# Early blocks of a routed expert network on one NeuronCore: two buffers for gathered rows and y, a ScalarE share of the rounding of h, copies of x one by one, other split of the early one-hots

## The reference

```python
z = _L0_cond_ref(x, cond_1024, L0_cond_weight)
logits = jnp.einsum('bsd,de->bse', z, Wr) + br
route_w = jax.nn.softmax(logits, axis=-1)
_, topk_idx = jax.lax.top_k(route_w, 2)
mask = jax.nn.one_hot(topk_idx, 8).sum(-2)
routed = route_w * mask
routed = routed / routed.sum(axis=-1, keepdims=True)
h = jax.nn.relu(jnp.einsum('bsd,edh->ebsh', z, W1) + b1[:, None, None, :])
expert_out = jnp.einsum('ebsh,ehd->ebsd', h, W2) + b2[:, None, None, :]
return x + jnp.einsum('bse,ebsd->bsd', routed, expert_out)
```

## Time and profile before

| what | value |
|---|---|
| median of 3 runs | 955.36 us |
| the profiled execution, its own time | 954.25 us |
| its span, first to last instruction | 952.4 us |
| PE busy | 891.8 us (94%) |
| DVE busy | 760.1 us (80%) |
| ACT busy | 560.0 us (59%) |
| POOL busy | 550.3 us (58%) |
| mean granted TensorE clock | 0.973 |

### The profile page before, as it was taken

How to read it: one execution, slowest core, us unless ns; L and a number is a source line. 1 busy time by engine, 2 the same in 40 slices (tenths; PEclk the granted TensorE clock), 3 DMA queues, 4 the chain that set the end, 5 groups by cost and what they waited for, 6 DMA issues and landing times.

```text
span 952.4 us, 20965 instructions
## 1 busy us (share of the span) xinstructions
PE 891.8 (94%) x6510; PEld 881.9 (93%) x6510; DVE 760.1 (80%) x1476; ACT 560.0 (59%) x971; POOL 550.3 (58%) x469
## 2 busy tenths in 40 slices
PE   4982799999999999999999999999999999999993
PEld 4981799998999999999999999999999999999993
DVE  3776589898998787887887878878878878888783
ACT  5854455557875655655656556556556565565561
POOL 6877154444444545665765656656657656566572
PEclk9995799999999999999999999999999999999997
DMA  7894845853443454423433343344234334244231
GB/s 247 286 335 182 287 102 111 252 134 79 96 128 91 90 134 91 85 48 89 89 85 94 49 95 83 45 94 88 47 88 89 56 82 90 51 89 88 46 45 22
DMA packets 52071, 104.25 MB, mean 109 GB/s; under 512 B 7104, under 2 KB 34272, under 8 KB 51264
## 3 DMA queue, kind: packets, MB, share of 16 engines
q0 software_dynamic: 27360, 38.36, 23.9%
q1 hardware_dynamic: 20544, 61.09, 19.5%
q10 hardware_dynamic: 4128, 4.33, 1.4%
HBM read 75.78 MB, written 36.35 MB: 118 GB/s over the span
## 4 chain that ended last, share of the span: by engine, by line
PE 81%; DVE 6%; DMA 4%; issue 3%; POOL 3%; ACT 1%; ACTq 1%; SPq 0%; DVEq 0%; POOLq 0%
PE psum L1412 13%; PE psum L1427 13%; PE psum L1426 13%; PE psum L1425 13%; PE psum L1414 12%; PE psum L1413 12%; PE psum L1391 2%; DMA z_row<-z_rows,idx_early 2%; POOL row_hot L532 1%; DMA x_buf<-in_xT 1%; DVE w_lo L1204 1%; PE psum L1309 1%; PE psum L1311 1%; PE psum L1310 1%; DVE h_hi L1245 1%
## 5 line engine op out<-in xcount | busy, mean ns | idle before, releaser
L764 ACT ACTIVATE h<-psum,b_all 128x384 f32<-128x384 f32 x376 | 218.0, 580 | 313.3 <-PE psum L1414 245.1
L1425 PE MATMUL psum<-w_hi,h_hi 128*128 128x256 f32 x1128 | 316.8, 281 | 4.6 <-DVE h_lo L1247 4.6
L1427 PE MATMUL psum<-w_hi,h_lo 128*128 128x256 f32 x1128 | 318.6, 282 | 0.0
L1426 PE MATMUL psum<-w_lo,h_hi 128*128 128x256 f32 x1128 | 316.9, 281 | 0.0
L1412 PE MATMUL psum<-z_hi,w_hi 128*128 128x384 f32 x752 | 259.0, 344 | 2.5 <-DVE z_lo L1210 2.0
L575 POOL DMA_INDIRECT out<-y,idx_put x102 | 226.1, 2216 | 49.1 <-POOL idx_put L571 26.7
L1414 PE MATMUL psum<-z_hi,w_lo 128*128 128x384 f32 x752 | 253.5, 337 | 0.0
L1413 PE MATMUL psum<-z_lo,w_hi 128*128 128x384 f32 x752 | 253.2, 337 | 0.0
L1204 DVE TENSOR_TENSOR w_lo<-raw,w_hi 128x1024 fp32r<-128x1024 f32 x190 | 232.7, 1225 | 22.8 <-ACT w_hi L705 22.7
L1247 DVE TENSOR_TENSOR h_lo<-h,h_hi 128x384 fp32r<-128x384 f32 x376 | 210.2, 559 | 13.0
L1425 PEld LDWEIGHTS psum<-w_hi,h_hi 128*128 128x128 f32 x1128 | 213.3, 189 | 6.6 <-DVE h_lo L1247 6.6
(11 more groups left out here) (198 smaller groups left out, 744.2 us busy)
## 6 DMA issues: line engine op xcount, KB each, us to landing
raw<-in_experts SPq DMA_DIRECT2D x64, 512.0 KB, 4.3
x_buf<-in_xT SPq DMA_DIRECT2D x16, 512.0 KB, 7.2
d_rep<-d_rows SPq DMA_DIRECT2D x4, 1056.0 KB, 7.0
z_rows<-z_all ACTq DMA_DIRECT2D x2, 2112.0 KB, 11.8
z_rows<-z_all SPq DMA_DIRECT2D x1, 2112.0 KB, 12.2
z_rows<-z_once SPq DMA_DIRECT2D x1, 2112.0 KB, 10.1
out<-y,idx_put POOLq DMA_INDIRECT x102, 4.7
z_row<-z_rows,idx_get POOLq DMA_INDIRECT x99
```

The costliest lines, as they stand in the source:

```text
L764: act.activation(h[c % NHP][:], h_ps[c % HP][:, 0:TB], ACT.Relu, bias=b1_all[:, ds(e, 1), c]).then_inc(s_relu, 1)
L1425: pe.matmul(yp, hi, w2(w_hi, c), start=(c == 0), stop=False)
L1426: pe.matmul(yp, hi, w2(w_lo, c), start=False, stop=False)
L1427: ins = pe.matmul(yp, lo, w2(w_hi, c), start=False, stop=(c == HC - 1))
```

## The change

Five edits, all about the time up to the end of the early blocks:

- `z_row` has two buffers for the early blocks. The gather of block 1 starts when that of block 0 has landed, and that of block b+2 when block b has been transposed and the gather of b+1 has landed.
- `y` has two buffers for blocks 0 to 12, so y of a block waits for the addition of the block two before.
- In chunks 3, 6 and 7 of blocks 0 to 12 ScalarE reads the product from PSUM twice: first it writes `h_hi`, rounded, then h. VectorE only makes `h_lo`.
- The five late copies of x wait for two gathers, and each for the copy before it.
- The one-hots of the early groups: VectorE 0, 1, 4, 6, 7 (was 0, 2, 6, 7), ScalarE 2 and 5 (was 4), GpSimd 3 (was 1, 3, 5). ScalarE copies its sums out after the column one-hots' input.

```diff
@@ -85,8 +85,9 @@
-    EARLY_ACT = (4,)
-    EARLY_POOL = (1, 3, 5)
+    EARLY_ACT = (2, 5)
+    EARLY_POOL = (3,)
+    ACT_HI = (3, 6, 7)
...
@@ -129,7 +130,7 @@
-        z_row = sb("z_row", [P, Q, ZW], f32)
+        z_row = [sb(f"z_row{i}", [P, Q, ZW], f32) for i in range(2)]
...
-        y = sb("y", [P, Q, D], f32, stage_b)
+        y = [sb("y0", [P, Q, D], f32, stage_b), y_other]
...
@@ -366,13 +369,25 @@
+        def row_of(b):
+            return z_row[b % 2] if is_early(b) else z_row[0]
+
+        def y_at(b):
+            return y[b % 2] if isinstance(b, int) and b < N1 - 1 else y[0]
+
+        def rows_here(eng, b):
+            eng.wait_ge(s_get, (b + 1) * (16 * Q))
+
+        def act_hi(b, c):
+            return isinstance(b, int) and b < N1 - 1 and c in ACT_HI
@@ -456,8 +471,9 @@
                 copy_x(i)
-            sp.wait_ge(s_get, 16 * Q)
+            sp.wait_ge(s_get, 2 * 16 * Q)
             for i in range(EARLY_COPIES, INIT):
+                sp.wait_ge(s_init, i * 16)
                 copy_x(i)
...
@@ -584,11 +600,14 @@
             fetch(0, idx_early, z_rows[0:T // 2, :])
+            pool.wait_ge(s_get, 16 * Q)
+            fetch(1, idx_early, z_rows[0:T // 2, :])
             for b in range(N1):
                 row_free(b)
-                if b + 1 < N1:
-                    fetch(b + 1, idx_early, z_rows[0:T // 2, :])
-                else:
+                if b + 2 < N1:
+                    pool.wait_ge(s_get, (b + 2) * 16 * Q)
+                    fetch(b + 2, idx_early, z_rows[0:T // 2, :])
+                if b + 1 == N1:
                     pool.wait_ge(s_idx, 2)
                     rows_written()
...
@@ -690,11 +709,14 @@
             row_hot_of(0)
-            for g in range(BG):
-                partial_of(g)
+            aways(1, 0, EARLY_ACT[1], 0)
+            aways(1, 0, EARLY_ACT[1], 1)
+            row_hot_of(1)
             for o in range(2):
                 for a in range(2):
                     col_of_of(0, o, a)
+            for g in range(BG):
+                partial_of(g)
             for g in range(BG, HG):
                 partial_of(g)
...
@@ -761,6 +783,10 @@
                     if not (fresh and c < NHP):
                         act.wait_ge(s_hlo, b * HC + c + 1 - back(c))
+                    if act_hi(b, c):
+                        act.wait_ge(s_h2, b * HC + c + 1 - NHX)
+                        act.activation(h_hi[c % NHX][:], h_ps[c % HP][:, 0:TB], ACT.Relu,
+                                       bias=b1_all[:, ds(e, 1), c]).then_inc(s_hhi_act, 1)
                     act.activation(h[c % NHP][:], h_ps[c % HP][:, 0:TB], ACT.Relu,
                                    bias=b1_all[:, ds(e, 1), c]).then_inc(s_relu, 1)
...
@@ -1213,18 +1242,18 @@
-                dve.wait_ge(s_put, (b + 1) * (16 * Q))
+                dve.wait_ge(s_put, (b if isinstance(b, int) and b < N1 - 1 else b + 1) * (16 * Q))
...
@@ -1242,8 +1272,13 @@
-                    dve.tensor_copy(h_hi[i][:], h[c % NHP][:]).then_inc(s_hhi, 1)
-                    dve.wait_ge(s_hhi, b * HC + c + 1)
+                    if act_hi(b, c):
+                        dve.wait_ge(s_hhi_act, b * len(ACT_HI) + ACT_HI.index(c) + 1)
+                        given += 1
+                    else:
+                        dve.tensor_copy(h_hi[i][:], h[c % NHP][:]).then_inc(s_hhi, 1 + given)
+                        given = 0
+                        dve.wait_ge(s_hhi, b * HC + c + 1)
                     dve.tensor_tensor(out=h_lo[i][:], in0=h[c % NHP][:], in1=h_hi[i][:].bitcast(f32),
```

More of the change, by code:

```diff
@@ L206, in bass_adaln_moe_ffn @@
         col_hot = sb("col_hot", [P, NTG, NSC], bf16, work)
+        y_other = sb("y_other", [P, Q, D], f32, work)
         past_late = sb("past_late", [P, MAXB + 1, NSEG], f32, work)
@@ L538, in fetch @@
                     pool.indirect_dma_start(
-                        out=z_row[:, q, :], out_offset=None, in_=rows,
+                        out=row_of(b)[:, q, :], out_offset=None, in_=rows,
                         in_offset=bass.IndirectOffsetOnAxis(ap=index[:, b * Q + q:b * Q + q + 1], axis=0)
@@ L552, in gather @@
                     pool.indirect_dma_start(
-                        out=z_row[:, q, :], out_offset=None, in_=z_rows,
+                        out=z_row[0][:, q, :], out_offset=None, in_=z_rows,
                         in_offset=bass.IndirectOffsetOnAxis(ap=idx_get[:, q:q + 1], axis=0)).then_inc(s_get, 16)
@@ L725, in second_half @@
                     act.wait_ge(s_negrow, 2)
-                    aways(1, 1, LATE_ACT[0], 0)
+                    aways(2, 1, LATE_ACT[0], 0)
                 if (b, c) == (5, 7):
-                    aways(1, 1, LATE_ACT[0], 1)
+                    aways(2, 1, LATE_ACT[0], 1)
                 if b == 6 and c in (0, 2):
@@ L731, in second_half @@
                 if (b, c) == (6, 3):
-                    row_hot_of(1)
+                    row_hot_of(2)
                 if (b, c) == (6, 6):
-                    aways(2, 1, LATE_ACT[1], 0)
+                    aways(3, 1, LATE_ACT[1], 0)
                 if (b, c) == (6, 7):
-                    aways(2, 1, LATE_ACT[1], 1)
+                    aways(3, 1, LATE_ACT[1], 1)
                 if (b, c) == (7, 3):
-                    row_hot_of(2)
+                    row_hot_of(3)
                 if (b, c) == (7, 6):
-                    aways(3, 1, LATE_ACT[2], 0)
+                    aways(4, 1, LATE_ACT[2], 0)
                 if (b, c) == (7, 7):
-                    aways(3, 1, LATE_ACT[2], 1)
+                    aways(4, 1, LATE_ACT[2], 1)
                 if (b, c) == (8, 3):
-                    row_hot_of(3)
+                    row_hot_of(4)
                 if b in (8, 9) and c in (0, 2):
@@ L996, in row_hot_of @@
                     dve.wait_ge(s_part, HG)
+                elif EARLY_DVE.index(g) >= HOT:
+                    dve.wait_ge(s_part, EARLY_DVE[EARLY_DVE.index(g) - HOT] + 1)
                 t = (g - r * HG) * TG
@@ L1215, in take_weights @@
                 e = expert_of(dve, b)
-                dve.wait_ge(s_get, (b + 1) * (16 * Q))
+                rows_here(dve, b)
                 if not fresh:
                     dve.wait_ge(s_rcur, b)
-                dve.tensor_copy(r_next[:], z_row[:, :, ds(e + D, 1)].rearrange("p q a -> p (q a)")).then_inc(s_rnext, 1)
+                dve.tensor_copy(r_next[:], row_of(b)[:, :, ds(e + D, 1)].rearrange("p q a -> p (q a)")).then_inc(s_rnext, 1)
             def y_of(b):
@@ L1236, in block_of_dve @@
             def block_of_dve(b, fresh):
+                given = sum(act_hi(b - 1, c) for c in (HC - 2, HC - 1)) if isinstance(b, int) and b >= 1 else 0
                 if not fresh:
@@ L1391, in transpose_z @@
                         ins = pe.transpose(zt_ps[c][:, q * P:(q + 1) * P].bitcast(f32r),
-                                           z_row[:, q, c * P:(c + 1) * P].bitcast(f32r), ident_r[:])
+                                           row_of(b)[:, q, c * P:(c + 1) * P].bitcast(f32r), ident_r[:])
                 ins.then_inc(s_zt, 1)
```

12 lines of the change are left out of this document (7 added, 5 removed).

## The result

The changed kernel takes **952.91 us** (median of 13 runs, 950.49 to 954.93); the kernel before now stands at 958.00 (13 runs, 954.86 to 959.34, among them the three shown above). The ratio is 0.9955, with an interval of 0.9943 to 0.9966: faster by 0.45%, where 947.4 us and a range of 943.5 to 952.0 were predicted. The direction is right. The time is 5.5 us above the forecast and just outside the range, though the medians of before have moved up by 2.6 us from the three first runs too.

What follows compares the result with a forecast made beforehand. TensorE, busy 94% of the span, bounds the kernel; only time before block 14 can be saved. 2.7 + 1.3 + 4.5 - 0.5 = 8.0 us off 954.25 gives 946.2; the median stands 1.1 higher: 947.4 us, range 943.5 to 952.

Steps and rivals of the forecast that it cites:

- Saved 2.7 us: Tables of the first half: moving early one-hots off GpSimd writes the indices at 87.6 instead of 90.28; bounds 1.5 to 3.0.
- Saved 1.3 us: Second gather, issued right behind the first, lands before block 0's chunk 7 needs it, ending TensorE's 1.32 us wait; 0 to 1.6.
- Saved 4.5 us net: Blocks 1 to 13: ScalarE takes 39 casts from VectorE, shortening TensorE's waits for VectorE's halves; between 1 and 7.
- Lost 0.5 us: Block 1: copies of x issued one by one delay the next expert's weights, making ScalarE's rounding 2.3 late; 0 to 1.7.
- about 1.8 is absorbed: Block 1: idle time of ScalarE and spare time of `h_lo` take up about 1.8 us of the 2.3 us weight delay.
- From block 14 on it never waits ... 17.43 us: Later blocks: TensorE never waits, transposes follow every 17.43 us, so time can come only from what lies before.
- a period from block 14 on other than 17.43: Sign that the prediction is wrong: later blocks' period differs from 17.43 us.
- the copies hold the weights back: Rival, early blocks: slower copies delay the weight load; a copy of 8.0 us makes it 12.2 late, 958 at 8.2; 4%.
- ScalarE takes VectorE's place: Rival, early blocks: ScalarE becomes late instead, so the rounding gives 0.5 in place of 4.5 us: 951.4; 18%.
- the bounds of the terms together: All terms at their ends: stated as 943.0 to 954.9 us, from which the range 943.5 to 952 was taken.

Runs made afterwards that it cites:

- eight copies ahead: Changed kernel with the second row buffer behind all other tensors and all eight copies of x issued ahead of the gathers: 952.26 us, ratio 0.9946.
- second trace of before: The kernel before, run again with no edit: 955.85 us, ratio 0.9987 to itself; the traced execution took 960.87 us.
- best kernel: Changed kernel with the second row buffer behind all other tensors and six of eight copies of x ahead of the gathers: 946.07 us, ratio 0.9888.
- second trace of the changed kernel: The changed kernel, run again with no edit beside the kernel before: 951.57 us, ratio 0.9945.
- a single y: Changed kernel with one y buffer as before the change, everything else as changed: 952.25 us, ratio 0.9945.
- split alone: Kernel before with only the new division of the early one-hots among the engines and the code that goes with it: 954.03 us, ratio 0.9969.
- buffer behind: Changed kernel with the second row buffer placed behind all other second-stage tensors, same instructions: 948.60 us, ratio 0.9909; two further runs add copies ahead.

## Why the prediction was wrong

The profiled pair differs by 1.3 us, where 8.0 were forecast. By TensorE's own borders the 6.7 between them are: 1.1 for the start of the tables, which is not the change's; 2.2 for block 1, which lost 2.7 where 0.5 were forecast; 1.2 for blocks 2 to 13; 0.7 for block 15, which took 18.16; 2.2 for the longer period of the blocks behind; and 0.4 in the rest. Block 0 gave 1.05 back: it gained 2.35 where 1.3 were forecast. That was luck in part, since its granted clock stood at half for 6.5 us in place of 8.3, and this stretch, from the first transposes on, varies from 5.2 to 8.3 us over the four profiles of the two kernels. Block 15 is long in one other profile, that with eight copies ahead (18.27), and in both TensorE waits for its gather:

```profile
377.03 0.71 PE L1426 MATMUL psum<-ident_r,z_row 128*128 128x128 f32 x6 [0.41 <-DMA z_row<-z_rows,idx_get]
```

The runs give the lasting part.

**"Saved 2.7 us" by the first one-hots: right.** The tables take 14.25 us in every run with the new split, 2.76 less. As forecast, ScalarE's queue is what is late next. `col_of` ends at 85.7, and the copies of the sums and the indices follow from it.

**"Saved 1.3 us" by the second gather: right in mechanism, undersized.** It was read from one execution. Its bounds were "between 0 and 1.6", but the second trace of before has 3.81 us of waiting and half a clock behind. The term has a tail that a single trace doesn't show. Subtracting the other measured terms from the difference of medians leaves some 3 us for it (5.1 less 2.8 and 4.2, and 2.5 and some 2.5 lost, both below); that is a remainder of terms that are each uncertain by a microsecond or more, not a measurement of its own.

**"Saved 4.5 us net" by ScalarE's share: right.** 4.25 us by medians within one group of runs. By blocks, before against the best kernel: 0.7 in block 2, 0.9 in 4, 0.8 in 5, 1.2 in 6 (forecast 0.8, 0.9, 1.1, 1.1), 0.2 in 8 (0.7), none in 9 (0.4). Block 3 lost 0.3 (0.5), which shows nothing: it took 18.53 in one execution of before and 19.05 in the other. Block 7 lost 0.5 and block 10 gained 0.6, neither of them forecast. Together blocks 2 to 13 gained 3.75.

**"Lost 0.5 us" by the copies: the first step that failed, by size.** The mechanism, the place and the waiting engine are right. The copies stood 5.36 apart (forecast 5.5; 101.66 to 123.11 in four), but the load landed 5.86 us after its issue and not 4.8, and ScalarE waited 3.47 us in place of 2.3:

```profile
130.74 1.06 ACT L727 ACTIVATE w_hi<-raw 128x1024 fp32r<-128x1024 f32 x1 [3.47 <-DMA raw<-in_experts]
```

The forecast took 4.8 from landings of 3.6 to 5.3 us; right behind a chain of copies three or four loads run at once, and the first of them landed after 5.54 to 6.46 in four profiles of this order. The third late copy, beside which the gather of block 3 runs, varied too: it held up the next for 5.29 us in the profiled execution, for 6.57 in the second trace of the changed kernel and for 7.24 in that with a single y. There ScalarE waited 4.48 and 5.68:

```profile
112.02 6.57 DMA out<-in_x
...
125.58 6.46 DMA raw<-in_experts
```

```profile
132.06 1.06 ACT L727 ACTIVATE w_hi<-raw 128x1024 fp32r<-128x1024 f32 x1 [4.48 <-DMA raw<-in_experts]
```

The second half of the miss is "about 1.8 is absorbed". Without a wait block 1 takes 17.43 to 17.51 on TensorE, as the forecast assumed. With waits of 2.92, 3.17, 3.47 and 4.48 it took 19.64, 19.31, 20.13 and 21.12, so only 0.8 to 1.3 of each was absorbed. A wait of 3.47 in place of 2.3, of which 0.9 and not 1.8 was absorbed, made 2.6 of the 0.5 in the profiled execution. By medians the copies behind the gathers cost **2.5 us** (948.60 against 946.07; 2.1 of it in TensorE's blocks 0 and 1), five times the forecast and above its bound of 1.7. The page "DMA: Bandwidth & Descriptors" of the Trainium skill, section Anatomy of one DMA, gave 4.4 us a copy by estimate. Its fit is for DMAs that GpSimd issues, and these copies are issued by SyncE, from DRAM to DRAM; measured, they took mostly 5.2 to 5.5. Its point, that single copies in a queue pay the fixed part each time, agrees with the traces: in the kernel before the five copies, issued together, landed from 103.55 to 116.76, 3.3 apart, though a gather ran among them, and one by one they stood 5.36 apart.

**"From block 14 on it never waits ... 17.43 us": the second step that failed.** But for block 15 above it still never waits, and its instructions are the same, but each block takes 17.50. The forecast called "a period from block 14 on other than 17.43" a sign of error and had no term for it, so the sum holds nothing for what a new buffer does to the tensors behind it. The second `z_row` moves all of them by 3168 bytes. That costs 0.06 to 0.07 us a block, 1.7 to 2.1 over blocks 17 to 46 and, as an estimate, **2 to 3 us** in all: 46 blocks at that price give 2.8 to 3.2, and two pairs of traces, with and without, differ by 1.7 and 2.4 over blocks 2 to 46. With it undone the changed kernel measured 948.6, and with the copies mended too 946.07, against a forecast of 947.4 (ratio 0.9888, forecast 0.9917). So the sum without these two misses was a little too careful.

Of the rivals, the slower side, "the copies hold the weights back", was this mechanism at a fourth of its price. "ScalarE takes VectorE's place" (951.4) would have given the right time for the wrong reason: the run without ScalarE's rounding excludes it. One slip in the working changes nothing: the bounds of the terms together give 943.8 to 954.6, not 943.0 to 954.9.

## What to carry to other kernels

A buffer added to a kernel that TensorE bounds can cost time, as here. Compare the period of the steady loop before and after, and if it has moved with no new wait, put the new buffer behind the operands rather than in front of them. Work that only has to be done some time, like these copies, belongs where the profile's DMA row is empty, with its amount measured: six copies fit here, eight cost 6 us. Where one engine runs ahead of another, a border between blocks read on the one is off for the other: y of block 0 hid 1.4 us of what block 1 lost. A short wait of TensorE costs more than its length when the granted clock falls behind it, and such a term should be read from more than one execution.

## What was not expected of the hardware

**The pace of the same products depends on where tensors lie in SBUF.** Period 17.43 to 17.45 with the old addresses (before twice, split alone, buffer behind three times), 17.50 to 17.51 with 3168 bytes more (six profiles), 17.55 with 3200. The starts of TensorE's products in blocks 19 to 44 show where it goes. The first products of chunk 7 and the second products of chunks 5 to 7 take the same in all, to 0.003 us, though their weights, z and h have all moved. The changed kernel loses 0.035 us a block in the first products of chunks 0 to 2 and 0.034 in the second products of chunks 0 to 3. Their weights lie ahead of the row buffers and have not moved, while z and h have. (The first products of chunk 3, of the same kind, gain 0.003.) With 32 bytes more these first products are back at their old pace, as the guess had it, but the second products of chunks 0 to 4 lose 0.088 and the first of chunks 4 to 6 lose 0.028. By what rule is open, and so is whether TensorE's own operands matter alone or together with what other engines read and write meanwhile.

**The granted clock halves at short waits, but not at each.** It fell to 0.5 during TensorE's wait of 3.81 us for a gather, for 6.8 us; 1.3 us behind its wait of 1.68, for 3.4; and at the end of its wait of 2.69 (behind ScalarE's of 5.68 for weights), for 3.4. At TensorE's waits of 1.12, 1.32 and 1.48 in this stage it stayed at 1.00. In the second trace of before TensorE started 20 instructions in the 4 us from 122, most of them at half clock, and 32 in the 4 us from 126, at full clock; so such a time costs up to half its length.
